# Expert weights read back from memory in pieces of 256 KB, one in flight, in place of 1 MB

## What is computed

```python
x = x + tanh(g_xattn) * attention(layernorm(x), ctx)      # 16 heads of 64, 64 keys per batch
xt = layernorm(x).reshape(4096, 256)
logits = xt @ gate_w.T                                    # 8 experts
w_topk, sel = top_k(logits, 2); w_topk = softmax(w_topk)  # two experts for each token
h = silu(xt @ w1[e]); y = h @ w2[e]                       # w1[e] 256x1024, w2[e] 1024x256
x = x + tanh(g_ffn) * sum over the two experts of w_topk * y
```

## Time and profile before

| | |
|---|---|
| median of 3 runs | 755.22 us (751.92 to 757.16) |
| the profiled execution | 754.83 us |
| its span, first to last instruction | 753.1 us |
| PE busy | 732.6 us, 97% of the span |
| DVE busy | 586.2 us, 78% |
| granted TensorE clock, mean | 0.993 |

### The profile page before, as it was taken

One profiled execution on the slowest core, in us unless ns is written; L12 is line 12 of the kernel. 1 busy time (PEld: TensorE's weight loads), 2 busy tenths in 40 slices (PEclk: granted clock), 3 DMA queues, 4 the chain that ended last, 5 costly groups with the idle time before them and its releaser, 6 DMA issues.

```text
span 753.1 us, 23502 instructions
## 1 busy us (share of the span) xinstructions
PE 732.6 (97%) x7992; PEld 607.2 (81%) x7993; DVE 586.2 (78%) x1273; ACT 374.8 (50%) x672; POOL 365.2 (48%) x309
## 2 busy tenths in 40 slices
PE   8899999999999999999899999999999999999996
PEld 7567767677767777767798898899999999999995
DVE  5788879898897979798777887767677767777672
ACT  4586777767677667654253332332333333333331
POOL 4135445767676766665333757332323333333333
PEclk9999999999999999999999999999999999999999
DMA  8452453536282725434787985334333433333332
GB/s 322 136 148 105 143 167 115 188 129 230 71 288 78 248 91 199 131 122 132 211 234 211 240 207 121 54 48 56 44 55 43 55 48 50 50 48 55 44 45 29
DMA packets 93182, 93.94 MB, mean 125 GB/s; under 512 B 59312, under 2 KB 77936, under 8 KB 92720
## 3 DMA queue, kind: packets, MB, share of 16 engines
q1 hardware_dynamic: 31040, 64.71, 25.6%
q0 software_dynamic: 13392, 18.03, 13.7%
q10 hardware_dynamic: 48672, 10.18, 7.7%
HBM read 53.89 MB, written 37.95 MB: 122 GB/s over the span
## 4 chain that ended last, share of the span: by engine, by line
PE 46%; DVE 2%; issue 2%; ACTq 1%; ACT 1%; another core or an unknown queue 1%; DMA 0%; DVEq 0%; POOL 0%; POOLq 0%
PE h_ps L1525 23%; PE pair_ps L1538 22%; ACTq L158 1%; DVE ht_l L1670 1%; DMA out<-y,meta 0%; ACT hid L1590 0%; DVE ht_h L1668 0%; ACTq L160 0%; ACT rec_odd L1615 0%; POOL out L1801 0%; PE h_ps L1569 0%; DVEq L1479 0%; PE last_job_ps L1556 0%; DVE last_stats L1698 0%
## 5 line engine op out<-in xcount | busy, mean ns | idle before, releaser
L1801 POOL DMA_INDIRECT out<-y,meta x71 | 127.3, 1793 | 232.2 <-ACT y L1597 199.8
L1525 PE MATMUL h_ps<-bx_h,w_now 128*128 128x128 f16 x2272 | 194.5, 219 | 1.8 <-issue 1.5
L1538 PE MATMUL pair_ps<-weights,ht_h 128*128 x1136 | 192.7, 274 | 2.5 <-issue 1.4
L1525 PEld LDWEIGHTS h_ps<-bx_h,w_now 128*128 128x128 f16 x2272 | 152.7, 98 | 6.8 <-issue 4.6
L1525 PE MATMUL h_ps<-bx_l,w_now 128*128 128x128 f16 x1136 | 156.4, 219 | 1.3 <-issue 1.3
L1538 PE MATMUL pair_ps<-weights,ht_l 128*128 x568 | 155.6, 274 | 0.0
L1538 PEld LDWEIGHTS pair_ps<-weights,ht_h 128*128 128x128 f16 x1136 | 110.5, 98 | 19.1 <-issue 4.0
L1597 ACT ACTIVATE y<-pair_ps,meta 128x256 f32<-128x256 f32 x71 | 33.7, 474 | 178.2 <-DMA out<-y,meta 102.1
L1668 DVE CAST ht_h<-hid 128x1024 f16<-128x1024 f32 x71 | 50.9, 717 | 87.5 <-ACT hid L1590 84.3
L1347 POOL TENSOR_TENSOR r_l<-r,r_h 128x512 f16<-128x512 f32 x62 | 75.6, 1219 | 69.6 <-ACT r_h L851 67.6
L1590 ACT ACTIVATE hid<-h_ps 128x1024 f32<-128x1024 f32 x71 | 72.7, 1024 | 73.3 <-PE h_ps L1525 64.5
(11 more groups left out here) (254 smaller groups left out, 1236.3 us busy)
## 6 DMA issues: line engine op xcount, KB each, us to landing
stage<-in_w SPq DMA_DIRECT2D x16, 1024.0 KB
w_split<-split SPq DMA_DIRECT2D x14, 1024.0 KB, 6.5
weights<-w_split SPq DMA_DIRECT2D x14, 1024.0 KB
rows<-records ACTq DMA_DIRECT2D x268, 32.0 KB
xin<-in_x SPq DMA_DIRECT2D x7, 512.0 KB, 5.8
x_even<-in_x SPq DMA_DIRECT2D x4, 512.0 KB
x_odd<-in_x SPq DMA_DIRECT2D x4, 512.0 KB
out<-x_even SPq DMA_DIRECT2D x4, 512.0 KB
```

Source lines behind the costliest of these rows:

```text
L1525: last = nc.tensor.matmul(h_ps[r % 2][:, c, :], w1_now[:, r % 2, s, k * F + c * P:k * F + c * P + P], xt[:, r % 2, k, :], start=(j == 0 an ...
L1538: last = nc.tensor.matmul(y_ps[r % 2], ht[:, r % 2, c, :], weights_at(e, s, WN // 2 + c * D, D).rearrange("p o n -> p (o n)"), start=(c == ...
L1801: pool.indirect_dma_start(out, bass.IndirectOffsetOnAxis(meta[:, r, 0:1].bitcast(U32), 0), y[:, r % 2, :], None, compute_op=ALU.add).then_ ...
```

## The change

One constant. Each of the two 1 MB loads of an expert becomes four loads of 256 KB; a load still has 256 contiguous runs, now of 1024 bytes in place of 4096. All of them go through the same loop, and each is waited for before the next is issued.

```diff
 FIRST = 2 * RB
-LOADS = 2
+LOADS = 8
 LEFT = 5
```

## The result

The changed kernel takes **822.11 us** (median of 4 runs, 817.63 to 823.81) against 755.05 us, a ratio of 1.0888 with a 95% interval of 1.0861 to 1.0916. The forecast was 788 us, 768 to 808: the direction held, the size did not. The profiled execution took 823.81 us with a span of 822.1, 69.0 us more than before.

The account below looks back on a forecast made before the run. The prediction took PE to bound the expert stage. To the profiled 754.8 us it added 31.4 for block 25 waiting on SP's late queue and 1.7 for the slower clock: 788 us, range 768 to 808.

Parts of the forecast that it names:

- The tail behind the last piece: On SP's queue after the last weights land: storing 512 rows, issuing eight pads and landing the last, together 11 us.
- the two short steps to PE: From the gate's opening to PE's start on block 25: two steps of 0.4 us each and signals, about 1.1 us.
- A quiet piece is 1.8 + 0.8 = 2.6 us: A 256 KB load on SP's queue while the engines stand still: 1.8 us fixed plus 0.8 for packets.
- the 3.0 us beside other traffic: Price taken for each 256 KB load on SP's queue while the engines work, between 2.8 and 3.8 us.
- The 1.8 us of fixed cost: Per load on SP's queue: 1.35 us from issue to first packet, some 0.4 after the last, unchanged by smaller pieces.
- the upper bound of a piece: A 256 KB load bearing a large load's whole excess of 1.3 us: 3.8 us, for which the sum gives 814 us.
- The clock: After PE's idle gap before block 25, a spell at 1.2 GHz in place of 2.4 was to add 1.7 us.
- The experts' first blocks: DVE's weight copies there: expert 1 3.1 us late, experts 2 to 5 in time, zero in the sum.
- the last part of the prediction: Signs to look for in the trace; PE pausing at each expert's first block, not once, would show the prediction wrong.
- Dear piece: Rival on SP's loads: the slowest engine makes a small piece cost 3.5 us, +49.3 + 1.7, 806 us; chance 0.13.
- Faster: Rival in the expert stage: small packets let other queues' transfers through, gaining up to 4.4 us, 750 us; chance 0.02.

## Why the prediction was right and wrong

**Right: who waits, and where it stops.** SP's queue ends late, ACT stands at its entry to the loop until the pads are through, and block 25 waits for it. The doubled 1 MB loads and the early pads show it, beside the trace. The tail behind the last piece was put at 11 us and measured 564.31 - 553.06 = 11.25; the two short steps to PE at 1.1 and measured 0.92.

**Wrong: the price of a piece.** The step that failed is "A quiet piece is 1.8 + 0.8 = 2.6 us", and with it the 3.0 us beside other traffic. Measured: 3.20 us with the engines standing, 3.74 while they work (40 issues from 352.0 to 497.7). 56 pieces took 201.1 us in place of 165.1: 36.0 us more, of which 1.2 came back because the loads began sooner. The other 34.8 are all that block 25 was later than forecast (66.2 us in place of 31.4). What the packets do in one quiet piece of the changed kernel, issued at 543.44 (packets from 543.5 to 544.7, then from 544.75 to 546.3 us):

```profile
DMA packets 0, 0.00 MB, mean 0 GB/s; under 512 B 0, under 2 KB 0, under 8 KB 0
```

```profile
q1 hardware_dynamic: 271, 0.26, 59.4%
```

The 1.8 us of fixed cost hold: 1.3 to the first packet, 0.4 behind the last. Between them lie some 1.5 us, not 0.8. The engines are busy on average 0.594 x 1.55 = 0.92 us each, so a packet takes 0.92 x 16 / 271 = 54 ns, not the 45 of the earlier trace rows; and the last packet ends some 0.5 us later than this busy time would need. The second was there to be seen in the first load: 3.2 us busy within 4.0 us. I put the whole gap between busy time and elapsed time down to other queues' traffic and let it vanish in the quiet. It does not vanish. In the kernel with doubled loads PE has no work after 508 us, and three 1 MB loads are issued there:

```profile
L1500 SPq DMA_DIRECT2D weights<-w_split x3: 517/518/518, 510.8 to 522.5; - x3
```

5.85 us each, against 6.31 on average: rest from other work gives back 0.46 us, not the 1.3 that I had charged to it. The prediction also read the earlier trace rows wrongly where it has the share of ACT's loads and GpSimd's adds rise from 0.77 to 0.88: these are the shares of all DMA traffic, the weights' loads included. Of what spreads the packets of a piece, the layout in main memory explains 0.13 us in the quiet and 0.24 beside other traffic (42 issues from 354.1 to 497.6, 3.50 us each); the rest stays open.

**Wrong: the range.** The text gave 3.8 us as the upper bound of a piece and 814 us for it, and then ended the range at 808. The measured 3.74 lay inside the first bound; the time lay outside even its 814, for the quiet pieces at the end were held at 2.6. A cost taken with two values needs both of them moved for the bound.

**The clock.** The term was 1.7 us and measured about 2.8. PE had stood idle for 50.1 us; from 566 to 570 us it had work without a pause and the granted clock was 0.50, the 1.2 GHz level:

```profile
566.00:570.00 4.00, 4.00 (x40) 4.00 (x38) 3.61 (x6) 0.77 (x2) 1.31 (x1) 0.50 0.23 35
```

The whole first layer of block 25 ran so, 5.30 us, where before, behind a stretch in which PE was busy 2.27 of 5 us, the low clock lasted 3.4 us by the prediction's working.

**The experts' first blocks.** Said to cost nothing, since the gate stands behind them. DVE waited 29.5 us there in five waits, and PE did pause at them, which the last part of the prediction had put down as a sign of error; it was one of the price, for at 3.74 us a piece eight take 29.9 us, longer than an expert's four or five blocks. At expert 1 DVE waited 11.4 us, where I had 3.1. The lateness was not made up before the gate: block 24 began at 509.68 in place of 493.67, and PE stood idle at the gate from 515 to 565 us, where I had 499 to 530. In the sum all this is nothing, as said, since SP's queue does not wait for it. They decide as soon as the gate is moved, as the early pads showed.

**The rivals.** "Dear piece" was the nearest (3.5 us, 806 us), with a chance of 0.13. "Faster" fell: the gate bound long before, and the 512 KB and 1 MB variants that leave it open differ from the kernel before by at most 0.24%, within their intervals. With packets of 1024 bytes only the kernel with pieces in flight left the gate open, and it was slower.

**The estimate from the Trainium skill.** Its page "DMA: Bandwidth & Descriptors" gives the fit in "Anatomy of one DMA — SWDGE (gpsimd) path" for DMAs that GpSimd issues, and the loads here are SP's. The estimate of 2.6 us for 256 KB lies 0.6 below the quiet piece here, and that of 4.4 us for 1 MB 1.45 below the quiet 5.85; the measurement decides. The advice of the Trainium skill in "Rules for kernel authors" of the same page is at least 1 MiB a DMA for bandwidth. With one load in flight the traces agree: 1 MB costs 6.3 us in one load, 10.2 in two, 14.4 in four and 22.0 in eight.

## What to carry to other kernels

Split a transfer on a queue that waits for each piece, and its whole turnaround is paid again for each: measure that from issue to next issue, in a stretch where nothing else moves, before scaling anything by bytes. Then look at what stands behind the transfers on the same queue, since what decides may be a small store that another engine waits for and not the data itself; moving that store ahead cost nothing here and took back half of the loss at 256 KB, all of it at 512 KB. Where elapsed time exceeds busy time of the DMA engines, do not take it for contention unless a quiet transfer shows that it goes away.

## What was not expected of the hardware

- A load with two runs for each partition takes 518 to 539 ns to issue, with 256 runs or with 64; one with a single run takes 320. At 256 and 512 KB that went with 0.39 and 0.72 us less for a load, at 1 MB with nothing (6.27 against 6.29).
- 256 KB for 32 partitions in 64 runs of 4 KB is slower (3.81 us) than for 128 partitions in 256 runs of 1 KB (3.60).
- Eight pieces of 256 KB in flight together took 12.0 us for 2 MB, two of 1 MB one after the other 12.6; yet the kernel with the pieces in flight was 0.8% slower, with one pause of 5 us on TensorE behind a late output add.
